# One transformer block in 3-pass fp32: projections and six up products with 512 columns a matmul, and splits and output norm at other steps

## What is computed

```
qkv = x @ Wqkv + bqkv;  q, k, v = split(qkv);  q, k centred over the features
q2 = normed(q*q) over the features;  k2 = normed(k*k) over the features, then over the rows
kv = k2^T @ v;  t2 = q2 @ kv / sqrt(N)
x1 = layernorm(x + (v + t2) @ Wln + bln)
sel = sigmoid(x1 @ expert_sel^T)                      (16 experts)
out = sum_e relu(x1 @ keys_e) @ values_e * sel_e      (keys_e 256x128, values_e 128x256)
result = layernorm(x1 + out)
```

## Time and profile before

| what | value |
|---|---|
| median of 3 runs | 1017.75 us (1017.37 to 1019.9) |
| the profiled execution | 1022.25 us, its span 1020.5 us |
| TensorE matmul, busy | 997.0 us (98%), 8324 matmuls |
| VectorE, busy | 812.0 us (80%) |
| ScalarE, busy | 529.2 us (52%) |
| GpSimd, busy | 210.7 us (21%) |
| DMA | 62.19 MB, mean 61 GB/s |
| share of TensorE in the chain that ended last | 85% |

### The profile page before, as it was taken

The page is one execution under the profiler, slowest core; times in us unless marked ns, Lnnn a source line. Parts: engine busy times, 40 slices in busy tenths (PEclk is TensorE's granted clock), DMA queues, the critical chain, the costliest instruction groups (busy, mean ns, idle before and its releaser), DMA issues.

```text
span 1020.5 us, 21965 instructions
## 1 busy us (share of the span) xinstructions
PE 997.0 (98%) x8324; PEld 984.7 (96%) x8324; DVE 812.0 (80%) x1874; ACT 529.2 (52%) x1150; POOL 210.7 (21%) x267
## 2 busy tenths in 40 slices
PE   7899999999999999999999999999999999999997
PEld 6789999999999999999999999999999999999997
DVE  4889887889768887798877888788887888778555
ACT  4566645566345653566445664456544566354323
POOL 0021112212222122221222112122211212122221
PEclk9999999999999999999999999999999999999999
DMA  5032111211122011220121311112111221111001
GB/s 184 22 113 75 44 43 62 88 62 43 43 99 90 22 44 63 84 94 32 44 73 54 105 43 43 63 54 94 43 43 62 83 66 43 43 65 42 23 2 42
DMA packets 47981, 62.19 MB, mean 61 GB/s; under 512 B 4098, under 2 KB 34562, under 8 KB 47876
## 3 DMA queue, kind: packets, MB, share of 16 engines
q1 hardware_dynamic: 47876, 60.79, 17.8%
HBM read 37.18 MB, written 23.07 MB: 59 GB/s over the span
## 4 chain that ended last, share of the span: by engine, by line
PE 85%; DVE 7%; ACT 3%; issue 2%; DMA 1%; SPq 0%; POOL 0%; DVEq 0%; ACTq 0%; POOLq 0%
PE up_bank L1333 31%; PE down_bank L1333 31%; PE ring_bank L1333 9%; PE qk_bank L1333 7%; PE g_bank L1333 3%; DVE x1T_l L959 1%; DVE gated_l L1103 1%; ACT z L642 1%; DVE gated L1097 1%; PE ring_bank L1584 1%; PE g_bank L1379 1%; PE ring_bank L1585 1%; ACT gated_h L560 1%; DVE qk L862 1%; DMA sel_rows<-sel 0%
## 5 line engine op out<-in xcount | busy, mean ns | idle before, releaser
L546 POOL PARTITION_BROADCAST sel_all<-sel_rows x240 | 196.1, 822 | 682.7 <-DVE gated L1097 615.7
L560 ACT ACTIVATE gated_h<-gated 128x512 fp32r<-128x512 f32 x256 | 161.5, 631 | 298.0 <-DVE gated L1097 294.4
L1333 PE MATMUL up_bank<-x1T_h,keys_h 128*128 128x256 f32 x1024 | 286.3, 280 | 2.1 <-DVE keys_l L1084 2.1
L1333 PE MATMUL down_bank<-vals_h,gated_h 128*128 128x256 f32 x1024 | 287.1, 280 | 0.3
L1333 PE MATMUL down_bank<-vals_l,gated_h 128*128 128x256 f32 x1024 | 286.2, 280 | 0.0
L1333 PE MATMUL down_bank<-vals_h,gated_l 128*128 128x256 f32 x1024 | 286.2, 280 | 0.0
L1333 PE MATMUL up_bank<-x1T_l,keys_h 128*128 128x256 f32 x1024 | 286.2, 279 | 0.0
L1333 PE MATMUL up_bank<-x1T_h,keys_l 128*128 128x256 f32 x1024 | 286.2, 279 | 0.0
L1103 DVE TENSOR_TENSOR gated_l<-gated,gated_h 128x512 fp32r<-128x512 f32 x256 | 172.2, 673 | 47.6 <-ACT gated_h L560 47.1
L1097 DVE SCALAR_TENSOR_TENSOR gated<-up_bank,sel_all 128x512 f32<-128x512 f32 x256 | 176.0, 688 | 39.5 <-PE up_bank L1333 34.9
L1333 PEld LDWEIGHTS up_bank<-x1T_h,keys_h 128*128 128x128 f32 x1024 | 194.0, 189 | 2.3 <-DVE keys_l L1084 2.3
(11 more groups left out here) (257 smaller groups left out, 1697.5 us busy)
## 6 DMA issues: line engine op xcount, KB each, us to landing
out<-z SPq DMA_DIRECT2D x32, 256.0 KB, 2.4
x_raw<-in_x SPq DMA_DIRECT2D x15, 512.0 KB, 4.8
xT_raw<-in_xT SPq DMA_DIRECT2D x14, 512.0 KB, 4.3
parked_q<-w_room SPq DMA_DIRECT2D x14, 512.0 KB, 2.6
q<-parked_q SPq DMA_DIRECT2D x56, 128.0 KB, 3.1
parked_x<-w_room SPq DMA_DIRECT2D x14, 512.0 KB, 2.6
w_room<-parked_x SPq DMA_DIRECT2D x56, 128.0 KB, 3.1
w_room<-in_keys SPq DMA_DIRECT2D x4, 512.0 KB, 4.5
```

The costliest lines, as they stand in the source:

```text
L546: nc.gpsimd.partition_broadcast(sel_all[:, e % 2], row, P).then_inc(sel_spread, 1)
L560: return nc.scalar.activation(dst, src, ACT.Copy, **kw)
L1333: last = mm(dst, lhs, rhs, start=start and i == 0, stop=stop and i == n - 1, **kw)
```

## The change

- The projection QK (eight row tiles a batch) is one product with 512 columns a matmul, 6 matmuls, where it was two halves of 256 columns with 6 each. The up product of the steps in WHOLE_UP (0, 3, 19, 21, 25, 28) is made the same way.
- In the table: QR of the second half goes from step 27 to 25, XR of the first half from 28 to 27, the two ZN of the first group from 26 and 27 to 29 and 30, and one bias of x from 30 to 27.
- The split of the key-weighted x (gT_h, gT_l) uses the room of x_h, x_l instead of that of k2_h, k2_l; the wait for kv_projected moves with it.

```
--- before.py
+++ after.py
@@ -45,12 +45,12 @@
         15: [("GG", 4), ("QK", 6), ("QS", 4)], 16: [("GG", 5), ("QS", 5)], 17: [("QK", 7)],
         18: [("ZA", 0), ("ZA", 1), ("QR", 0), ("GG", 6)], 19: [("KS", 0), ("GG", 7), ("QS", 6)], 20: [("KV", 0), ("QS", 7)],
         21: [("Y", 0)], 22: [("Y", 1), ("XS", 0)], 23: [("Y", 2), ("XS", 1)], 24: [("Y", 3), ("XS", 2)],
-        25: [("XS", 3)], 26: [("ZN", 0)], 27: [("QR", 1), ("ZN", 1)], 28: [("XR", 0)], 30: [("LG", 0)],
+        25: [("QR", 1), ("XS", 3)], 27: [("XR", 0)], 29: [("ZN", 0)], 30: [("ZN", 1), ("LG", 0)],
     },
 
 
     split_xT={4: 0, 9: 1}, split_x={5: 0, 10: 1, 13: 2, 16: 3},
-    bias_x={9: 0, 14: 1, 30: 2, 31: 3},
+    bias_x={9: 0, 14: 1, 27: 2, 31: 3},
 
     gpsimd_xT=(), gpsimd_x=())
 FIRST_PLAN = {
@@ -63,6 +63,7 @@
             gpsimd_xT=(), gpsimd_x=())
 LAST_STEPS = 3
 ROWS_STEP = 14
+WHOLE_UP = (0, 3, 19, 21, 25, 28)
 ROW_ROOMS = 3
 LAST_ROWS_STEP = 4
 BLOCK = 32
@@ -132,7 +133,6 @@
         wvl_h, wvl_l = sb("wvl_h", [P, M, C], F32R), sb("wvl_l", [P, M, C], F32R)
         kvw_h, kvw_l = sb("kvw_h", [P, M, C], F32R), sb("kvw_l", [P, M, C], F32R)
         k2_h, k2_l = sb("k2_h", [P, 2, C], F32R), sb("k2_l", [P, 2, C], F32R)
-        gT_h, gT_l = k2_h, k2_l
         ident, ones = sb("ident", [P, P]), sb("ones", [P, P])
 
 
@@ -141,6 +141,7 @@
         gated_h, gated_l = sb("gated_h", [P, HELD, GN], F32R), sb("gated_l", [P, HELD, GN], F32R)
         xT_h, xT_l = sb("xT_h", [P, G, M, GN], F32R), sb("xT_l", [P, G, M, GN], F32R)
         x_h, x_l = sb("x_h", [P, 2, C], F32R), sb("x_l", [P, 2, C], F32R)
+        gT_h, gT_l = x_h, x_l
         qT_h, qT_l = sb("qT_h", [P, 2, 2, M, P], F32R), sb("qT_l", [P, 2, 2, M, P], F32R)
         esel_h, esel_hl = sb("esel_h", [P, M, P], F32R), sb("esel_hl", [P, M, P], F32R)
         q2, x1 = sb("q2", [P, T, C]), sb("x1", [P, T, C])
@@ -576,6 +577,8 @@
                     at_least(act, x_in[i // 2], it * 16 + 16)
 
                     at_least(act, g_added, k_tile(it + 1, 2 * i - 1))
+                    if i == 0:
+                        at_least(act, kv_projected, it)
                     copy(x_h[:], x_raw[:, 2 * i:2 * i + 2]).then_inc(x_hi, 1)
 
             def squares(it, b, t):
@@ -601,7 +604,6 @@
                 act.wait_ge(k_scaled, n)
 
                 at_least(act, g_added, n - 2)
-                at_least(act, kv_projected, b - 1)
                 copy(k2_h[:, t % 2], k2[:, t % 2], scale=k_scale[:, t % 2:t % 2 + 1]).then_inc(k_hi, 1)
 
                 at_least(act, k4_summed, n - 1)
@@ -1514,13 +1516,9 @@
                         pe.wait_ge(xT_lo, k_half(b, h))
 
                         at_least(pe, qk_biased, k_tile(b, a) - 1)
-                        for half_of in range(2):
-                            cols = slice(half_of * C, (half_of + 1) * C)
-                            last = product(qk_bank[:, cols],
-                                           [(both(xT_h, xT_l, ALL, h, m, slice(i * P, (i + 1) * P)),
-                                             both(wqk_h, wqk_l, ALL, m, cols)) for m in range(M)],
-                                           start=half_of == 0, skip_group_check=True)
-                        last.then_inc(qk_projected, 1)
+                        product(qk_bank[:], [(both(xT_h, xT_l, ALL, h, m, slice(i * P, (i + 1) * P)),
+                                              both(wqk_h, wqk_l, ALL, m, ALL)) for m in range(M)],
+                                start=True).then_inc(qk_projected, 1)
                     elif kind == "GG":
                         pe.wait_ge(k_lo, k_tile(b, a))
                         pe.wait_ge(x_lo, k_pair(b, a // 2))
@@ -1596,13 +1594,18 @@
                         pe.wait_ge(piece_lo, 2 * (e // 4) + 1)
 
                     at_least(pe, gate_applied, f - 1)
-                    for half_of in range(2):
-                        cols = slice(half_of * QUARTER, (half_of + 1) * QUARTER)
-                        last = product(up_bank[s % 2][:, cols],
-                                       [(both(keys_h, keys_l, ALL, e, m, ALL),
-                                         both(x1T_h, x1T_l, ALL, g, m, cols)) for m in range(M)],
-                                       start=half_of == 0, skip_group_check=True)
-                    last.then_inc(up_made, 1)
+                    if s in WHOLE_UP:
+                        product(up_bank[s % 2][:], [(both(keys_h, keys_l, ALL, e, m, ALL),
+                                                     both(x1T_h, x1T_l, ALL, g, m, ALL)) for m in range(M)],
+                                start=True).then_inc(up_made, 1)
+                    else:
+                        for half_of in range(2):
+                            cols = slice(half_of * QUARTER, (half_of + 1) * QUARTER)
+                            last = product(up_bank[s % 2][:, cols],
+                                           [(both(keys_h, keys_l, ALL, e, m, ALL),
+                                             both(x1T_h, x1T_l, ALL, g, m, cols)) for m in range(M)],
+                                           start=half_of == 0, skip_group_check=True)
+                        last.then_inc(up_made, 1)
                 layer1(it, s)
                 if (it, s) == (0, 0):
                     queries0(3)
```

5 lines of the change are left out of this document (2 added, 3 removed), and 2 rows, old and new, of the table plan.

## The result

The changed kernel takes **1032.43 us** (median of 4 runs, 1028.69 to 1035.25); the kernel before took 1017.56 beside it (4 runs, 1016.64 to 1019.9). The ratio is 1.014, with a 95% interval of 1.010 to 1.018: slower, where the prediction said 1011.5 us and not above 1026. The profiled execution took 1032.9 us, half a microsecond above its median; that of before (1022.25) lies 4.7 above its own, so the two traces show 10.65 of the 14.9 us between the medians.

What follows compares the result with a forecast made beforehand. TensorE was taken to bound the kernel, by its two matmul paces and few waits. Terms -0.3 - 10.8 + 5.0 = -6.1 us took the profiled 1022.25 to 1016.15, and the median to 1011.5 us; range 1003 to 1026.

Steps and rivals of the forecast that it cites:

- Wider matmuls: Projections and six up products: 624 pairs of 256 columns become 624 matmuls of 512, -0.3 us, nothing directly.
- the pace of the rest: Remaining 256-column matmuls run more often at 113.3 ns than 117.8: -10.8 us, bounds +6.4 and -16.4.
- A: Part of each of seven batches from its first down product to the start of up product 27.
- Its rule: A block of six 512s turns slow to fast in half the cases and leaves fast when entered fast.
- The last batch: Without a next batch to work on, its fast share goes from 0.48 to about 0.77: 0.9 us gained.
- the 230 to 236 forecast: Sign to look for: the six 512s of a block start 230 to 236 ns apart.
- Steps 25 to 2: Batch end, led by a chain through other engines: late gate rows delay z, +5.0 us, bounds -3.7 and +10.
- the wait for z: Before the down product of step 0, TensorE stalls 1.0 us until VectorE has added the finished output.
- B: Rest of each of seven batches, from up product 27 to the next batch's first down product.
- The logits' wait: Before the logits of step 30, TensorE's wait for x1T_l goes: 0.53 us in each of seven batches.
- The rivals: Blocks toss a coin 1018.5 us (0.18); locked slow 1029 (0.12); rows do not bind 1003 (0.12); nothing gained 1022.5 (0.13).
- Rows bind, locked slow: Blocks of six always leave slow and gate rows come late: +6.4, +5.0 and -0.3, 1029 us, chance 0.12.

Runs made afterwards that it cites:

- e3: Kernel before with only the 512-column matmuls and the other room for the key-weighted x, step table unchanged: 1014.0 us, ratio 0.992.
- e7: Kernel before with q's split at step 25, x1's split and the bias at 27, no wide matmul: 1005.7 us, ratio 0.980.
- e11: Kernel before with one edit, the second half of q split at step 25 instead of 27: 1005.43 us, ratio 0.987.
- e1: Changed kernel with only the first group's output norm put back to steps 26 and 27: 1002.57 us, ratio 0.981.
- e6: e1 without the six wide up products, projections still at 512 columns: 1005.04 us, ratio 0.980.
- e10: e7 with the up product of step 21 alone as 512-column matmuls: 997.27 us, ratio 0.979.
- e4: Changed kernel with the logits put ahead of the second norm in step 30, norms still at 29 and 30: 1022.71 us, ratio 1.001.
- e5: Changed kernel with 18 further matmuls in step 2 of batches 1 to 7: 1025.11 us, ratio 1.000; unaltered beside it 1031.81 us.
- e12: Kernel before with the change's whole step table and no wide matmul: 1029.95 us, ratio 1.011.
- e2: Kernel before with only the first group's output norm moved to steps 29 and 30: 1023.97 us, ratio 1.002.

## Why the prediction was wrong

By its own steps, in microseconds of the profiled execution: forecast -6.1, measured +10.65.

*Wider matmuls, -0.3, and the pace of the rest, -10.8.* In the batches A was to change by -10.2. Measured is -4.6, of which four falls of the clock are 4 x 1.55 = +6.2, so the pace gave -10.8 there. This term held: the fast share forecast for steps 3 to 24 was 0.755, from 0.25, and counted by intervals it is 0.77, from 0.28. Its rule held by half. Of the blocks of six entered fast at the full clock, 64 of 68 left fast; of those entered slow, only 3 of 15, not half. (Of the two fast entries that the rule rested on, one, at 104.1 us, lies ahead of the 110 us from which the entries were counted; it does stand in the trace.) That the share came out all the same is in part luck: five of the seven batches were fast from step 4 on and stayed so, and one was slow through all its blocks up to step 19. The last batch, forecast -0.9, came out +0.7, and that was not followed up. The 512s start 225 to 236 ns apart, 232.5 on average, with the first interval of a block entered fast at 226, below the 230 to 236 forecast; the isolated gap of 216 ns that the Trainium skill (TensorE: Matmul & The Clock Gate, Back-to-back issue gap) gives for 512 columns was seen in no run.

But the credit was one-sided. The prediction gave the pace to the wide blocks. They do bring it, if the logits still wait (e3: -0.8%). The earlier split of q brings as much and more (e7: -2.0%, e11: -1.3%), and what all the wide blocks add then is under the noise of ratios between groups (e1, e6 and e7 agree within 0.1%), while the one at step 21 alone adds 0.8% (e10 against e11).

*Steps 25 to 2, +5.0: the step that failed.* It came to +14.3: the wait for z that was to be 1.0 us of standing was 2.05 to 2.45 us between starts. Against the chain as forecast (the changed trace's times less 6.34, by which its gate 25 at 530.88 lies behind the 524.54 of before):

```profile
551.49 0.69 DVE L1099 SCALAR_TENSOR_TENSOR gated<-up_bank,sel_all 128x512 f32<-128x512 f32 x1
...
559.46 1.28 DVE L997 TENSOR_TENSOR z<-down_bank,x 128x512 f32<-128x512 f32 x2
```

```profile
554.30 1.73 SPq L454 DMA_DIRECT2D sel_rows<-sel  x3
```

```profile
556.58 1.46 POOL L547 PARTITION_BROADCAST sel_all<-sel_rows  x2 [4.28 <-DMA sel_rows<-sel]
```

Gate 31 is 0.25 later than I had it, the rows are issued 0.25 later and used 0.55 later, z is added 0.6 later, and TensorE starts another 0.15 behind that: each link was named, each a little short, 0.75 in sum. Over seven batches that makes 5.3 us. Another 1.1 us is only in the counting: TensorE reaches up product 27 some 0.16 us sooner at the fast pace, but the chain's end does not move, so A's gain is paid back in B. The last 2.8 us come from two batches of 27.4 and 26.6 us, against 25.6 on average in the other five. In the first of them x1's block is read back late:

```profile
406.57 0.33 SPq L439 DMA_DIRECT2D parked_x<-w_room  x1
411.04 2.52 SPq L445 DMA_DIRECT2D w_room<-parked_x  x4
...
532.15 0.33 SPq L439 DMA_DIRECT2D parked_x<-w_room  x1
534.77 2.52 SPq L445 DMA_DIRECT2D w_room<-parked_x  x4
```

```profile
416.07 1.15 ACT L561 ACTIVATE x1T_h<-w_room 128x512 fp32r<-128x512 f32 x2 [3.61 <-DMA w_room<-parked_x]
```

The read is issued 4.47 us behind the store ahead of it, where it is 2.62 at the other batch end; in the second, at 781, the read itself lands a microsecond later. In the kernel before, the split was a step later, and the longest such delay at a batch end, 3.00 us, left no mark on B (23.85, as its neighbours). I had priced the landing at its median and left its spread out of the bounds. And e4 shows that the chain forecast was not the only one: with the rows in time, the end of the batch was nearly as long. I had found nothing late on ScalarE and VectorE ahead of the rows ("None of these is late"); there the norms' own work is what binds next.

*What was not in the sum at all*: the clock, +6.2 in this trace. I had written down a new wait of 1.0 us on TensorE and taken its length as its whole price. With a wait of that length it would have been: none of the gaps of 1.3 us in e4 brought the clock down.

*The logits' wait, -0.53 a batch.* It went, as forecast; without the late norm its end is worth far more, by the pace of the steps behind it (e11). The prediction had noticed that the pace was slow after a wait "in nearly every case", though by its own rows four of these seven waits left the stream fast, and did not ask what the end of the wait would do.

*The rivals.* None took place. "Rows bind, locked slow" gave 1029, near the time, by a pace that did not occur.

Of the 10.65 us: B is 9.3 above its forecast, the clock 6.2, the last batch 1.6, the start 0.3, and the pace 0.6 better; 9.3 + 6.2 + 1.6 + 0.3 - 0.6 = 16.8, the distance from -6.1. The remaining 4.2 us between the medians lie in the profiled execution of before, which was slower than its median.

Open is why the clock fell behind some waits and not behind others of the same length, and why some of the blocks that are entered slow turn fast: in all the traces, without a wait ahead, 53 of 161 of six 512s and 42 of 47 of four did. Those whose 512s start 236, 236, 231, 236 ns apart leave fast and those 231, 229, 236, 231 apart stay slow, but that pattern may be the pace itself and not its cause, and what fixes it was not tried.

## What to carry to other kernels

Price a new wait of the busiest engine by more than its length: look at the granted clock in narrow windows behind it, and at the pace in which the stream goes on; and price the end of an old wait the same way. Before moving work later to make room, follow each engine's queue behind it for two steps: the split that was really in the way (q's) could be moved earlier, and that alone gained 14 us. When one chain is cleared, look for the next one behind it before counting the gain (e4). Where several edits come as one, undo each alone: here one of them (the norm) cost 2.4 to 3.4%, another (the split of q) gave 1.3 to 2%, and what the one that stood first in the description gave beside it was too small for these runs to settle.

## What the chip showed that I had not expected

- Removing a wait of 0.53 us from each of seven batches (e11) took 11 us from the parts A, where only step 25 was touched. Some 10 of them are pace: 2304 more of the 256-column matmuls in A start at the fast distance, 4.4 ns less each.
- TensorE gained 6.7 us from 126 additional matmuls (e5), put where it waited.
- The granted clock fell to its lower level behind 7 of 14 gaps of 2.05 to 2.59 us between starts (the changed kernel's two traces), behind none of 7 of 2.28 to 2.54 (e12's trace), none of 7 of 1.9 to 2.0 (e2) and none of 7 of 1.3 (e4). Each fall lasted 3.4 us and cost 1.55.
- A matmul of 512 columns (232.5 to 233.8 ns on average, by kernel) costs more than two of 256 at the fast pace (226.7) and less than two at the slow one (235.6 to 235.8), in every kernel.
- A block of six 512s that found the stream fast left it fast in 601 of 621 cases, over all traces; one that found it slow left it fast in 53 of 161.
